# Gather phase of a graph layer: earlier first gathers, eight sets of message buffers, accumulator filled by ScalarE

## The reference

```python
xn = layernorm(x)
HW = xn @ W                                     # h_table, 12500 x 256
msgs = edge_weight[:, None] * HW[dst]           # 200000 edges
x = x + segment_sum(msgs, src, 12500) + b \
      + linear_attention(xn, Wq, Wkv, Wproj) + bproj
x = x + top2_of_8_experts(layernorm(x))         # 256 -> 512 -> 256 each
# linear_attention: q = elu(xn Wq) + 1, k = elu(xn Wk) + 1, v = xn Wv
#   context = sum over nodes of k^T v;  out = (q context) / (q . sum k)
```

## Time and profile before

| | |
|---|---|
| median of 3 runs | 4451.63 us (4451.18 to 4458.18) |
| profiled execution | 4446.43 us, its span 4444.5 us |
| sort and join | until 824 us |
| gather phase, first gather to last add | 831 to 3320 us |
| POOL L729 in it | 1660 gathers, 1583.3 us busy |
| PE busy in it | 1637.67 of 2489 us |

### The profile page before, as it was taken

One profiled execution on the slowest core, in us unless ns is written; L12 is line 12 of the kernel. 1 busy time (PEld: TensorE's weight loads), 2 busy tenths in 40 slices (PEclk: granted clock), 3 DMA queues, 4 the chain that ended last, 5 costly groups with the idle time before them and its releaser, 6 DMA issues.

```text
span 4444.5 us, 56780 instructions
## 1 busy us (share of the span) xinstructions
PE 3140.5 (71%) x16504; PEld 2560.2 (58%) x16505; DVE 2597.7 (58%) x6324; ACT 604.6 (14%) x1276; POOL 2537.1 (57%) x2437
## 2 busy tenths in 40 slices
PE   5767665566666666665676666666645379999998
PEld 5756554344545545544555555555535368888887
DVE  8887775444544544545767767667655145444444
ACT  8112221100000000000000000000001112222221
POOL 0057777466666666666666666666642447744444
PEclk9987777778778777778888888888875579999999
DMA  6666664533333333333333333333376235644443
GB/s 191 219 185 193 198 188 132 152 101 101 101 99 102 100 99 101 101 97 110 112 112 108 111 107 112 111 109 113 99 106 199 73 67 120 122 78 72 72 71 57
DMA packets 363112, 522.66 MB, mean 118 GB/s; under 512 B 69240, under 2 KB 282748, under 8 KB 363004
## 3 DMA queue, kind: packets, MB, share of 16 engines
q0 software_dynamic: 130944, 275.64, 25.7%
q1 hardware_dynamic: 181523, 190.28, 14.4%
q10 hardware_dynamic: 50537, 55.32, 4.0%
HBM read 378.21 MB, written 140.28 MB: 117 GB/s over the span
## 4 chain that ended last, share of the span: by engine, by line
PE 30%; another core or an unknown queue 17%; DVE 16%; issue 12%; DVEq 5%; DMA 2%; POOL 0%; ACT 0%; SPq 0%; ACTq 0%; POOLq 0%
PE bank L1422 9%; PE bank L1435 9%; DVE acc L1817 7%; PE bank L1230 6%; DVE select L1810 5%; DVEq L56 2%; PE bank L1333 2%; PE bank L1365 2%; DVEq L1817 1%; DVE relu_kq L1904 1%; PE bank L1409 1%; PE bank L1331 1%; DMA read_back<-lists 1%; PE bank L1357 1%
## 5 line engine op out<-in xcount | busy, mean ns | idle before, releaser
L729 POOL DMA_INDIRECT message<-h_table,gather_stage x1660 | 1583.3, 954 | 928.6 <-issue 505.9
L1817 DVE TENSOR_TENSOR acc<-acc,bank 128x256 f32 x1660 | 697.4, 420 | 880.5 <-remote 636.9
L1230 PE MATMUL bank<-message,select 128*128 128x256 f32 x3320 | 976.6, 449 | 294.5 <-issue 165.1
L1230 PEld LDWEIGHTS bank<-message,select 128*128 128x128 f32 x3320 | 726.2, 227 | 530.7 <-issue 245.7
L689 POOL DMA_INDIRECT lists<-placed,dest_i x300 | 374.3, 1248 | 375.7 <-ACT placed L911 281.2
L783 POOL DMA_INDIRECT out<-acc,row_of x224 | 351.3, 1568 | 341.3 <-DVE acc L2110 266.7
L1810 DVE TENSOR_SCALAR select<-iota_n,gather_stage 128x128 f32<-128x128 f32 x1660 | 467.3, 359 | 3.5
L1236 PE MATMUL bank<-w_cat,xt_in 128*128 128x256 f32 x784 | 257.1, 442 | 229.6 <-issue 228.7
L1422 PE MATMUL bank<-fx_t,acc 128*128 128x256 f32 x1792 | 411.8, 383 | 10.1 <-DVEq L2062 4.7
L1435 PE MATMUL bank<-w,acc 128*128 x1792 | 405.6, 379 | 2.7 <-issue 2.7
L1422 PEld LDWEIGHTS bank<-fx_t,acc 128*128 128x128 f32 x1792 | 344.9, 193 | 59.0 <-DVEq L2062 5.0
(11 more groups left out here) (299 smaller groups left out, 3848.8 us busy)
## 6 DMA issues: line engine op xcount, KB each, us to landing
rows<-block_dram SPq DMA_DIRECT2D x75, 514.5 KB
acc<-x_sorted SPq DMA_DIRECT2D x112, 260.0 KB
message<-h_table,gather_stage POOLq DMA_INDIRECT x1660
xt_in<-xt_dram SPq DMA_DIRECT2D x98, 256.0 KB
x_sorted<-blank_rows ACTq DMA_DIRECT2D x42, 390.0 KB
lists<-zeros_list SPq DMA_DIRECT2D x8, 1664.0 KB, 15.4
read_back<-lists SPq DMA_DIRECT2D x13, 1024.0 KB, 5.7
x_sorted<-blank_rows SPq DMA_DIRECT2D x2, 6370.0 KB
```

The costliest lines, as they stand in the source:

```text
L729: pool.indirect_dma_start(out=message[:, slot % SETS, j, :], out_offset=None, in_=h_table, in_offset=Offset(ap=gather_stage[:, slot, j, 0: ...
L1230: last = nc.tensor.matmul(ps, select[:, slot % 2, j, :], message[:, slot % SETS, j, :], start=True, stop=True)
L1817: added = V.tensor_tensor(to, to, ps, ALU.add)
```

## The change

Five things are changed together.
- Eight sets of message buffers (`RING`) in place of four: set k waits for set k-8, no longer for set k-4. They take the SBUF space of other arrays, some of which move into the end of `acc`.
- SP stages the first two turns after the first decoded part (one segment), inside the join, so POOL's first gathers begin there. `PARTS` are now 1, 4, 4 and 4 segments.
- ACT fills `acc` in 14 copies between its copies of the join; POOL's 7 copies are gone.
- The matmuls for `tile_row`, the turning of the weights and their copies move ahead, into the join.
- DVE writes a lane of weight 0 with its own lane's number as the row to gather, by two more operations for each part.

The staging of later turns is unchanged: turn t still waits until turn t-2 is aggregated.

```diff
-    PART_MAX = 5
+    PART_MAX = 4
...
+        acc_flat = acc[:, :, :].rearrange("p b c -> p (b c)")
+        LENT = NB // 7 - 3
+        lent = acc_flat[:, 7 * LENT * CR:NB * CR]
+        w_nat = lent[:, 0:8 * C].rearrange("p (a c) -> p a c", c=C)
+        bias_in = lent[:, 8 * C:10 * C].rearrange("p (a c) -> p a c", c=C)
+        iota_tile = lent[:, 10 * C:10 * C + TC]
+        past_tile = lent[:, 10 * C + TC:10 * C + TC + TC // 2].bitcast(BF16)
+        assert 10 * C + TC + TC // 2 <= 21 * CR
...
+        message = sb("message", [P, RING, SET, C], F32, early)
+        lane = sb("lane", [P, 1], F32, early)
...
-        message = sb("message", [P, SETS, SET, C], F32, early)
...
-        PARTS = [(0, 1), (1, 4), (4, 8), (8, RSEG)]
+        PARTS = [(0, 1), (1, 5), (5, 9), (9, RSEG)]
...
                 if seg >= 2:
                     sp.wait_ge(s_join_psum, seg - 1)
                 bring_list(seg)
+                if seg == 3:
+                    sp.wait_ge(s_records, 1)
+                    for half in range(2):
+                        stage_list(half, half)
             sp.wait_ge(s_records, len(PARTS))
-
-            def stage_list(turn, half):
-                first_tile = turn * SETS * SET if isinstance(turn, int) else sp.snap(turn * (SETS * SET))
-                sp.dma_start(gather_stage[:, half * SETS:(half + 1) * SETS, :, :].rearrange("p s j w -> p (s j) w"),
-                             records[:, ds(first_tile, SETS * SET), :]).then_inc(s_list[half], 16)
 
             def bring_xt(pair, half):
                 sp.dma_start(xt_in[:, half, :, :].rearrange("p k n -> p (k n)"),
                              xt_dram[ds(pair, 1), :, :].rearrange("a p n -> p (a n)")).then_inc(s_xt_in[half], 16)
-            for half in range(2):
-                stage_list(half, half)
             bring_xt(PAIRS - 1, 0)
...
-            for a in range(0, NB, 14):
-                acc_made = pool.tensor_copy(acc[:, a:a + 14, 0:C], bias_row[:, :].unsqueeze(1).to_broadcast([P, 14, C]))
-            acc_made.then_inc(s_late, 1)
+            pool.engine_nop().then_inc(s_late, 1)
 
             def gather_set(slot):
                 pass_gate()
                 for j in range(SET):
                     pool.indirect_dma_start(
-                        out=message[:, slot % SETS, j, :], out_offset=None, in_=h_table,
-                        in_offset=Offset(ap=gather_stage[:, slot, j, 0:1], axis=0)).then_inc(s_message[slot % SETS], 16)
+                        out=message[:, slot, j, :], out_offset=None, in_=h_table,
+                        in_offset=Offset(ap=gather_stage[:, slot, j, 0:1], axis=0)).then_inc(s_message[slot], 16)
             for slot in range(RING):
                 pool.wait_ge(s_list[slot // SETS], 16)
-                if slot >= SETS:
-                    pool.wait_ge(s_agg, slot - SETS + 1)
                 gather_set(slot)
             with pool.Fori(1, TSETS // RING) as i:
                 for slot in range(RING):
                     pool.wait_ge(s_list[slot // SETS], i * 16 + 16)
-                    pool.wait_ge(s_agg, i * RING + (slot - SETS + 1))
+                    pool.wait_ge(s_agg, i * RING + (slot - RING + 1))
                     gather_set(slot)
             for slot in range(TSETS % RING):
                 k = TSETS // RING * RING + slot
                 pool.wait_ge(s_list[slot // SETS], TSETS // RING * 16 + 16)
-                pool.wait_ge(s_agg, k - SETS + 1)
+                pool.wait_ge(s_agg, k - RING + 1)
                 gather_set(slot)
...
+            def copy_weights():
+                for i in range(4):
+                    act.wait_ge(s_wt_psum, i + 1)
+                    ps = bank[i][:, :].rearrange("p (k a n) -> p k a n", k=KC, a=2)
+                    into = [w_cat[:, :, 2 * C:3 * C], w_cat[:, :, 0:C], w_cat[:, :, C:2 * C], wp_t[:, :, :]][i]
+                    act.activation(into.rearrange("p k (a n) -> p k a n", a=2), ps, ACT.Copy).then_inc(s_wt, 1)
+
+            def fill_acc(piece):
+                act.activation(acc[:, 7 * piece:7 * piece + 7, 0:C], bias_row[:, :].unsqueeze(1).to_broadcast([P, 7, C]),
+                               ACT.Copy).then_inc(s_acc_made, 1)
             join(0)
             for seg in range(RSEG):
                 if seg + 1 < RSEG:
                 act.wait_ge(s_back_psum, seg + 1)
                 act.activation(found_bf[:, seg * P:(seg + 1) * P, :],
                                bank[4 + seg % 2][:, :].rearrange("p (c t) -> p t c", c=PIECES), ACT.Copy).then_inc(s_back_out, 1)
-
-            for i in range(4):
-                act.wait_ge(s_wt_psum, i + 1)
-                ps = bank[2 + i][:, :].rearrange("p (k a n) -> p k a n", k=KC, a=2)
-                into = [w_cat[:, :, 2 * C:3 * C], w_cat[:, :, 0:C], w_cat[:, :, C:2 * C], wp_t[:, :, :]][i]
-                act.activation(into.rearrange("p k (a n) -> p k a n", a=2), ps, ACT.Copy).then_inc(s_wt, 1)
+                if seg == 1:
+                    act.wait_ge(s_late, 3)
+                if seg == 6:
+                    copy_weights()
+                if seg:
+                    fill_acc(seg - 1)
+            for piece in range(RSEG - 1, NB // 7):
+                fill_acc(piece)
...
+            pe.wait_ge(s_past, 1)
+            for i in range(-(-TC // 512)):
+                n = min(512, TC - 512 * i)
+                nc.tensor.matmul(bank[i][0:1, 0:n], ones_bf[0:NB, 0:1], past_tile[0:NB, 512 * i:512 * i + n],
+                                 start=True, stop=True).then_inc(s_tile_psum, 1)
+
+            def turn_weights():
+                pe.wait_ge(s_tile_row, -(-TC // 512))
+                pe.wait_ge(s_wload, 16 * 3)
+                for i in range(4):
+                    for k in range(KC):
+                        for a in range(2):
+                            last = nc.tensor.transpose(bank[i][:, (k * 2 + a) * P:(k * 2 + a + 1) * P],
+                                                       w_nat[:, 2 * i + a, k * P:(k + 1) * P], ident[:, :])
+                    last.then_inc(s_wt_psum, 1)
             join(0)
             for seg in range(RSEG):
                 if seg + 1 < RSEG:
                     join(seg + 1)
+                if seg == 5:
+                    turn_weights()
...
                 pe.wait_ge(s_select, k + 1)
                 if first:
-                    pe.wait_ge(s_message[slot % SETS], slot // SETS * 64 + 64)
+                    pe.wait_ge(s_message[slot], 64)
                 else:
-                    pe.wait_ge(s_message[slot % SETS], (k - slot % SETS) * 16 + 64)
+                    pe.wait_ge(s_message[slot], (k - slot) * (64 // RING) + 64)
                 if not (first and slot < 2):
                     pe.wait_ge(s_added, k - 1)
                 for j in range(SET):
                     ps = bank[(slot % 2) * 2 + j // 2][:, (j % 2) * C:(j % 2 + 1) * C]
-                    last = nc.tensor.matmul(ps, select[:, slot % 2, j, :], message[:, slot % SETS, j, :], start=True, stop=True)
+                    last = nc.tensor.matmul(ps, select[:, slot % 2, j, :], message[:, slot, j, :], start=True, stop=True)
...
+                steps.done(V.tensor_tensor(records[:, part, 2], fb, fa, ALU.bitwise_or))
+                steps.settle()
+
+                steps.done(V.tensor_scalar(fa, records[:, part, 2].bitcast(F32), 0.0, lane[:, 0:1], ALU.is_equal, ALU.mult))
+                steps.settle()
+                V.tensor_tensor(records[:, part, 0], records[:, part, 0], fa, ALU.max).then_inc(s_records, 1)
...
+            dve.wait_ge(s_acc_made, NB // 7)
```

More of the change, by code:

```diff
@@ L243, in gps_layer @@
         found_b = sb("found_b", [P, PART_MAX * P], I32, inputs)
-        iota_tile = sb("iota_tile", [P, TC], F32, inputs)
-        past_tile = sb("past_tile", [P, TC], BF16, inputs)
-        w_nat = sb("w_nat", [P, 8, C], F32, inputs)
-        bias_in = sb("bias_in", [P, 2, C], F32, inputs)
         inputs.close()
+        mix_w = sb("mix_w", [P, KC, C], F32, early)
+        ksum = sb("ksum", [P, KC, P], F32, early)
+        ctx_t = sb("ctx_t", [P, KC, P], F32, early)
+        ctx = sb("ctx", [P, KC, P], F32, early)
         xt_in = sb("xt_in", [P, 2, KC, 2 * P], F32, early)
@@ L372, in gps_layer @@
         s_list = [sem(f"s_list{i}") for i in range(2)]
-        s_message = [sem(f"s_message{i}") for i in range(SETS)]
+        s_message = [sem(f"s_message{i}") for i in range(RING)]
+        s_acc_made = sem("s_acc_made")
         s_select = sem("s_select")
@@ L402, in gps_layer @@
         s_y_out = sem("s_y_out")
-        acc_flat = acc[:, :, :].rearrange("p b c -> p (b c)")
         fx_end, hid_n = 2 * UNIT_RING * CR, 2 * KH * 2 * P
@@ L504, in _, with stage_list @@
             sp.dma_start(bias_in[:, 1, :], mix_bproj.partition_broadcast(P)).then_inc(s_first_w, 16)
+            def stage_list(turn, half):
+                first_tile = turn * SETS * SET if isinstance(turn, int) else sp.snap(turn * (SETS * SET))
```

(31 more changed lines are left out.)

5 lines of the change are left out of this document (1 added, 4 removed).

## The result

The changed kernel takes 4920.82 us in the median (4870.43 to 4923.16), the kernel before 4451.63: ratio 1.101, 95% interval 1.090 to 1.112. It is slower by 10%, in the forecast's direction and inside its range, but by 469 us where 278 were forecast (4730 - 4451.6).

A forecast was written before the change was run, and what follows sets the result against it. PE's signals held during POOL's long gather rows were taken to bound the gather phase; +127 context, +160 mixing, 0 start, 0 `acc` fill, -10 lanes gave +277: 4723 us profiled, 4729 median (own range 4640 to 4800; stated range 4370 to 4950).

The forecast's parts named there:

- What bounds the phase: Gather phase, 2489 us: PE's signals given late in POOL's row of back-to-back gathers are heard only some 3.3 us after it.
- held span: From 10 us into a row of POOL's gathers to 3 us behind it, when PE's signals were claimed not to pass.
- Buffers hide next to nothing, and the list stands in the way: Eight buffer sets: PE waits only 11.4 us for messages; each turn now waits for SP's list, some 3.1 us.
- Context turns: 53 turns with context or sets only: 26.1 us each in place of 23.7, +127 us.
- Mixing turns: 49 turns with mixing: 27.1 us each against 23.85, +160 us, bounds +110 and +203.
- Rows of 32: Rival: both lists staged early, POOL runs 32 gathers in a row; +500 us, 4940 us; chance 0.13.
- The start: First gathers 47 us earlier, at 784, but their row holds the join's signals: 0 us, bounds -33 and +30.
- Lanes of weight 0: Last sets, where such lanes all read row 0: PE's sets 5.0 us apart instead of 6.5; -10 us, between 0 and -16.

The follow-up runs named there:

- a_break: Changed kernel plus a POOL wait before each turn's third set until the second set's gathers have landed: 4620.73 us against 4452.08 for the kernel before, ratio 1.038.
- w4_send: a_wait4 with POOL's row of 84 sends broken by a wait for landing after each 8: 4371.06 us against 4452.08 for the kernel before, ratio 0.981.
- w4_send16: w4_send with the pauses after each 16 sends instead of 8, on another kind of chip: 3943.00 us against 3969.14 for the kernel before, ratio 0.993.
- w4_late_send: w4_send with the first lists staged behind all decoded parts, on the other kind of chip: 3963.90 us, ratio 0.999 to the kernel before.
- a_wait4: Changed kernel with eight buffer sets, but POOL waits again for set k-4: 4424.82 us against 4449.86 for the kernel before, ratio 0.995.
- a_wait2: As a_wait4, but POOL waits for set k-2: 4444.40 us, ratio 0.998 to the kernel before.
- a_send16: Changed kernel with the row of 84 sends broken after each 16: 4988.88 us against 4490.59 for the kernel before, ratio 1.110.

## Why the prediction was right, and where it was off

- *What bounds the phase* was right: signals of PE that are heard only after POOL's row. a_break, w4_send and the join show it in three places, and the chip without it bears out what it costs: there the phase from first gather to last add is 2149 us (748.0 to 2897.1, w4_send16), against 2521 for the same code in the phase on a chip with it (w4_send) and 2488 before. Behind the last add the two kinds of chip are alike, 1054.3 us (w4_late_send) and 1057.0 (w4_send), both with breaks after 8 sends. The Trainium skill's rule that engines are independent, and a matmul does not block another engine unless a semaphore stands between them (Trainium Architecture — The Big Picture, "What this means for kernel authors"), fits the traces of that one chip (adds 0.2 us behind the matmuls, no idle time inside PE's groups). In the others it does not hold of POOL's indirect DMAs: PE's matmuls inside a group wait for no semaphore, and stand 234.5 us idle beside them.
- *The held span's bounds* were read from rows of 16 to 24 gathers and are rough. The delay grows from about 6 us into a row on; the shown add is released 1.4 us behind its row; and in the row of 84 sends, which the prediction took for a confirmation, signals pass in the middle and the last comes 11 us behind.
- *Buffers hide next to nothing, and the list stands in the way*: right. 11.4 us of waits for messages went, 96 of POOL's pauses end with the list. a_wait4 gives all of the loss to the deeper wait, on a chip with the held span.
- *Context turns* were right in mechanism and close in size: 25.7 us for 26.1.
- *Mixing turns* are the step that failed, a term of the sum that was mis-sized: +160 us forecast, bounds +110 and +203, measured +370. I counted PE's work by the open time that it has today, 15.0 us, as if it could be poured into any open span. The timeline shows a chain instead: row of gathers, held add, `act_kq`, L1342, the last set, the list. The shown turn adds up as 20.0 + 9.0 + 2.6 = 31.6 us, and the order of the chain could have been read from the program.
- *Rows of 32* came only three times after the first (as 1 and 31), so this rival did not happen, though its time of 4940 is nearest to the result. Rows of 16 made it, with pauses of 5.5 us in context and 12.9 in mixing (medians).
- *Luck*: 4921 lies outside the forecast's own range of 4640 to 4800. It is inside the stated range only because that range was drawn out to 4950 for the rows of 32.
- *The start*: 0 forecast, +6.9 measured; the first gather came at 789.1 (784 forecast) and the join ended near 857, where 854 was forecast.
- *Lanes of weight 0*: -10 forecast, -9.8 measured between turn 103's start and the last add. No run had this part alone.
- *Only one kind of chip* was in view. The prediction took the held span for a property of the kernel's traffic; it is one of the chip that runs it too. That the changed kernel's loss needs the held span is not shown: it was not run on the other kind of chip.

## What to carry to other kernels

Before buffers are deepened, look at who waits for what is buffered: 11 us of waits were all that there was to hide, and what the depth moved was where the issuing engine pauses. Where a wait is taken away, the next one in line (here the list) sets the pace, and work that hangs on a round trip between engines must be followed as a chain, not as an amount. And check whether a delay is the same on a second chip before tuning around it: a pause of 2.5 us a turn won 300 us in one kernel on one chip and lost 263 in another kernel on another.

## What the runs showed of the hardware

- On at least three of the chips used, signals from PE to other engines came late while POOL issued indirect DMAs back to back: the adds that VectorE waited for by 7.5 us in the median in the kernel before and 8.5 in the changed one, there by up to 34 us, and ScalarE's copies after waits of up to 37 us in the sends. On one they came 0.2 us after the matmuls, in rows of any length. The kernel before takes 4450 to 4490 us on the ones and 3969 on the other. Why the chips differ stays open.
- Where signals are late, PE itself is slow too: inside groups of matmuls that wait for nothing it is idle 234.5 us in w4_send, with starts 2.1 us apart, and 0.0 us in w4_send16 on the other chip. So what is held is more than a signal on its way; whether it is PE's finishing of its matmuls, which the trace only models, or the delivery of its instructions stays open.
- POOL's pauses free the signals from some length on: 2.5 us in rows of 10 and 20 us did (a_break), 1.7 to 2.6 in rows of 10 us did (w4_send), 0.59 did not in the one place looked at (a_wait2), 1.8 in rows of 20 us did not reliably (a_send16).
- POOL's long copies did not hold PE: beside the 21.89 us of copies of `acc` in the kernel before the join's signals from PE to ScalarE passed promptly, as here, 0.3 us after the matmuls' end (782.02):

```profile
781.63 0.39 PE L1198 MATMUL bank<-ident_bf,joined 128*128 128x128 bf16 x4
...
782.32 0.59 ACT L949 ACTIVATE found<-bank 128x512 bf16<-128x512 f32 x1
```
